# A recurrence in blocks of 24 steps, with the input products beside every step

## The reference, cut to what matters

```python
def cell(h, x):
    gi = x @ W_ih + b_ih
    gh = h @ W_hh + b_hh
    i_r, i_z, i_n = jnp.split(gi, 3, axis=-1)
    h_r, h_z, h_n = jnp.split(gh, 3, axis=-1)
    r = jax.nn.sigmoid(i_r + h_r)
    z = jax.nn.sigmoid(i_z + h_z)
    n = jnp.tanh(i_n + r * h_n)
    h_new = (1.0 - z) * n + z * h
    return (h_new, h_new)
```

## Time and profile before

| | us |
|---|---|
| median of 3 runs | 2068.12 (2065.51 to 2073.94) |
| the profiled execution | 2068.51 |
| its span in the profile | 2066.7 |
| TensorE busy | 1857.9 (90%) |
| recurrence: first gate matmul to the next stage's first matmul | 1138.73 to 2011.40 |

### The profile page before, as it was taken

One profiled execution on the slowest core, in us unless ns is written; L12 is line 12 of the kernel. 1 busy time (PEld: TensorE's weight loads), 2 busy tenths in 40 slices (PEclk: granted clock), 3 DMA queues, 4 the chain that ended last, 5 costly groups with the idle time before them and its releaser, 6 DMA issues. The chain is left out here.

```text
span 2066.7 us, 86137 instructions
## 1 busy us (share of the span) xinstructions
PE 1857.9 (90%) x32542; PEld 1377.3 (67%) x32542; DVE 1257.9 (61%) x5543; ACT 1097.8 (53%) x4105; POOL 377.3 (18%) x1398
## 2 busy tenths in 40 slices
PE   8877998999989989899888899999998999999876
PEld 4234454463644646455556898989898989999875
DVE  5545383654835447363343677777777777777766
ACT  0342736636355363645644565656565655656554
POOL 3000000000000000000000334343434333333335
PEclk7788999999999999999999796969797988879556
DMA  5222213222032220413223000000000000000002
GB/s 175 77 78 53 79 29 94 66 55 87 20 105 56 71 89 1 117 28 73 72 62 108 1 1 0 0 0 0 0 0 0 0 0 0 0 0 0 0 0 82
DMA packets 103527, 86.76 MB, mean 42 GB/s; under 512 B 15616, under 2 KB 90496, under 8 KB 103440
## 3 DMA queue, kind: packets, MB, share of 16 engines
q1 hardware_dynamic: 101392, 84.38, 14.2%
q10 hardware_dynamic: 1664, 1.18, 0.2%
q0 software_dynamic: 384, 0.01, 0.0%
HBM read 60.20 MB, written 21.00 MB: 39 GB/s over the span
## 5 line engine op out<-in xcount | busy, mean ns | idle before, releaser
L1255 PE MATMUL bank_pair_A<-moving,rep 128*128 128x16 f16 x8192 | 327.7, 172 | 55.3 <-DVE moving L1494 49.5
L1255 PEld LDWEIGHTS bank_pair_A<-moving,rep 128*128 128x128 f16 x8192 | 277.8, 99 | 75.6 <-DVE moving L1494 59.1
L1255 PE MATMUL bank_pair_C<-moving,rep 128*128 128x16 f16 x8192 | 321.8, 171 | 0.0
L1255 PE MATMUL bank_pair_B<-moving,rep 128*128 128x16 f16 x8192 | 321.7, 171 | 0.0
L1352 ACT ACTIVATE r_gate<-r_pre 128x16 f32<-128x16 f32 x512 | 110.4, 216 | 301.7 <-DVE r_pre L1443 301.7
L1255 PEld LDWEIGHTS bank_pair_C<-moving,rep 128*128 128x128 f16 x8192 | 266.3, 99 | 0.0
L1255 PEld LDWEIGHTS bank_pair_B<-moving,rep 128*128 128x128 f16 x8192 | 266.3, 99 | 0.0
L1242 PE MATMUL bank_pair_D<-x_part,w_in 128*128 128x256 f16 x1536 | 213.1, 288 | 6.0 <-ACT gi_rz L1379 3.5
L1443 DVE TENSOR_REDUCE r_pre<-bank_pair_A 128x16 f32<-128x32 f32 x512 | 98.1, 192 | 151.5 <-PE bank_pair_A L1255 151.5
L1137 POOL TENSOR_TENSOR x<-x,w_in 128x512 f32<-128x512 f32 x8 | 10.2, 1274 | 964.7 <-DMA w_in<-w_in 964.7
L1043 DVE TENSOR_REDUCE head_max<-bank_pair_A 128x2 f32<-128x1024 f32 x128 | 155.9, 1218 | 38.3 <-PE bank_pair_A L579 38.1
(11 more groups left out here) (260 smaller groups left out, 3632.0 us busy)
## 6 DMA issues: line engine op xcount, KB each, us to landing
rep<-parts SPq DMA_DIRECT2D x256, 64.0 KB
parts<-parts SPq DMA_DIRECT2D x48, 256.0 KB, 2.1
q_rep<-parts SPq DMA_DIRECT2D x32, 256.0 KB, 4.5
k_rep<-parts SPq DMA_DIRECT2D x64, 128.0 KB, 2.8
w_in<-in_x_dram SPq DMA_DIRECT2D x8, 512.0 KB, 4.2
x<-in_x_dram SPq DMA_DIRECT2D x8, 512.0 KB, 4.4
parts<-parts SPq DMA_DIRECT2D x32, 128.0 KB, 2.6
out_dram<-res SPq DMA_DIRECT2D x16, 256.0 KB, 2.1
```

Of the source, the lines that this page charges most:

```text
L1255: last = nc.tensor.matmul(ps[part][:, o:o + 2 * B], w[:, k, (first + c) * P:(first + c) * P + P], moving[j % 2][:, k, :, :].rearrange("p s ...
```

## The change

A block is now TS = 24 steps, which is exactly the 24 steps over which 12 groups spread; ten such blocks (FULL = 10) and 16 last steps (LAST = 16) make up the 256. Every step of the ten blocks carries a product: eight matmuls of 192 columns (24 tokens x 8) while the next block has 24 tokens, and of 128 columns in the tenth block, whose products are for the last 16 steps. Each step's product is followed by one matmul on constant operands (`steady`), 256 columns, into an otherwise unused bank; each of the last 16 steps, which have no product, is followed by eight of them. The split of x is made two blocks ahead, into one of two buffers chosen by the block's parity, in 8 pieces of 96 elements on the 16 r and z steps; the first two blocks' splits are made before the recurrence begins, on ScalarE and VectorE. GpSimd's wait for a moved n group remains once a block, behind the last group. The three inner loops run over groups 0 to 7, 8 to 10, and 11. The last two full blocks are written out after the outer loop of eight.

```diff
+    BODY = 2
+    TS = MC * BODY
+    FULL, LAST = N // TS, N % TS
...
-        x_part = t("x_part", [P, 2, DC, B, TB], F16)
+        x_part = t("x_part", [P, 2, 2, DC, B, TS], F16)
...
-        pG = [pD[:, 0, 0:B * TB], pD[:, 1, 0:B * TB]]
-        BLOCKS = N // TB
-        BODY = 2
-        PLAIN = TB - MC * BODY
+        pG = [pD[:, 0, 0:B * TS], pD[:, 1, 0:B * TS]]
...
+        def buffer_of(n):
+
+            return n % 2
+
+        def x_half(n, part, k, width):
+
+            return x_part[:, bass.ds(buffer_of(n), 1), part, :, :, :].rearrange("p o c b t -> p (o c) (b t)")[:, k, 0:B * width]
+
         def blocks(eng, step, product):
 
-
-            with eng.Fori(0, BLOCKS - 1) as blk:
-                with eng.Fori(0, PLAIN // BODY) as k:
-                    for j in range(BODY):
-                        step(blk * TB + k * BODY + j, j, blk, True, k)
-                with eng.Fori(0, RZ) as m:
-                    for j in range(BODY):
-                        step(blk * TB + m * BODY + (PLAIN + j), j, blk)
-                        product(blk + 1, m, j, False)
-                with eng.Fori(RZ, MC) as m:
-                    for j in range(BODY):
-                        step(blk * TB + m * BODY + (PLAIN + j), j, blk)
-                        product(blk + 1, m, j, True)
-            with eng.Fori(0, TB // BODY) as k:
+            def run(q, made, split):
+
+                for low, high in ((0, RZ), (RZ, MC - 1), (MC - 1, MC)):
+                    with eng.Fori(low, high) as m:
+                        for j in range(BODY):
+                            step(q * TS + m * BODY + j, j, (q + 2, m, split) if split and low == 0 else None)
+                            product(q + 1, m, j, (low >= RZ) + (high == MC), made)
+
+            with eng.Fori(0, FULL - 2) as q:
+                run(q, TS, TS)
+            run(FULL - 2, TS, LAST)
+            run(FULL - 1, LAST, None)
+            with eng.Fori(0, LAST // BODY) as k:
                 for j in range(BODY):
-                    step(k * BODY + (N - TB + j), j, BLOCKS - 1, True)
+                    step(k * BODY + (FULL * TS + j), j)
+                    product(FULL + 1, None, j, False, 0)
 
...
-            def products(m, k, bank):
+            def products(n, m, k, bank, width):
 
                 for w in range(2):
                     for part in range(2):
-                        last = nc.tensor.matmul(bank, w_in[w][:, k, bass.ts(m, P)], x_part[:, part, k, :, :].rearrange("p b t -> p (b t)"),
+                        last = nc.tensor.matmul(bank[:, 0:B * width], w_in[w][:, k, bass.ts(m, P)], x_half(n, part, k, width),
                                                 start=(k == 0 and w == 0 and part == 0), stop=(k == DC - 1 and w == 1 and part == 1))
                 return last
...
+            def steady(times):
+                for n in range(times):
+                    nc.tensor.matmul(pD[:, 1, 0:2 * P], w_in[0][:, n % DC, 0:P], w_in[1][:, n % DC, 0:2 * P], start=True, stop=True)
+
+            def product(n, m, j, is_n, width):
+                if not width:
+                    return steady(8)
                 if j == 0:
-                    pe.wait_ge(x_lo, blk * DC + DC)
-                    pe.wait_ge(gi_out, blk * MC + m)
+                    pe.wait_ge(x_lo, n * RZ + RZ)
+                    pe.wait_ge(gi_out, n * MC + m)
                 for k in range(j * DC // BODY, (j + 1) * DC // BODY):
-                    last = products(m, k, pG[0])
+                    last = products(n, m, k, pG[0], width)
                 if j == BODY - 1:
                     last.then_inc(gi_ps, 1)
+                steady(1)
...
-            for k in range(DC):
-                nc.scalar.activation(x_part[:, 0, k, :, :], xT[:, k, :, 0:TB], ACT.Copy).then_inc(x_hi, 1)
+            for n in range(2):
+                for k in range(DC):
+                    nc.scalar.activation(x_part[:, n, 0, k, :, :], xT[:, k, :, n * TS:(n + 1) * TS], ACT.Copy).then_inc(x_hi, 2)
...
-            def split(blk, k, j):
-
-                src = xT[:, bass.ds(k, 1), :, bass.ts(blk, TB)].rearrange("p o b t -> p (o b) t")
-                hi, lo = (x_part[:, n, bass.ds(k, 1), :, :].rearrange("p o b t -> p (o b) t") for n in range(2))
+            def split_of(n, m, width, j):
+
+                src = xT[:, :, :, bass.ds(n * TS, width)].rearrange("p c b t -> p (c b) t")[:, bass.ds(m * (B // 2), B // 2), :]
+                at = m // 2 * (B * TS) + buffer_of(m) * (B // 2 * width)
+                hi, lo = (x_part[:, bass.ds(buffer_of(n), 1), part, :, :, :].rearrange("p o c b t -> p (o c b t)")[:, bass.ds(at, B // 2 * width)]
+                          .rearrange("p (b t) -> p b t", b=B // 2) for part in range(2))
                 if j == 0:
                     nc.gpsimd.tensor_copy(hi, src).then_inc(x_hi, 1)
                 else:
-                    pool.wait_ge(x_hi, blk * DC + k + 1)
+                    pool.wait_ge(x_hi, n * RZ + m + 1)
                     nc.gpsimd.tensor_tensor(lo, src, hi, ALU.subtract).then_inc(x_lo, 1)
 
             def input_n(step):
...
-                if k is not None:
-                    split(blk + 1, k, j)
+                if split:
+                    split_of(*split, j)
...
-            def product(blk, m, j, is_n):
-                if j == BODY - 2 and is_n:
-
-                    pool.wait_ge(gi_out, blk * MC + m + 1)
+            def product(n, m, j, is_n, width):
+                if j == BODY - 2 and is_n == 2:
+
+                    pool.wait_ge(gi_out, n * MC + m + 1)
```

More of the change, by code:

```diff
@@ L1171, in recurrence @@
         bhh_c = t("bhh_c", [P, MC])
-        later = gi_rz[:, TB:N, :, :].rearrange("p t m b -> p (t m b)")
+        later = gi_rz[:, TS:N, :, :].rearrange("p t m b -> p (t m b)")
         staged = later[:, 0:DC * 3 * D].rearrange("p (c n) -> p c n", c=DC)
@@ L1294, in first_products @@
                     if m == 0:
-                        pe.wait_ge(x_lo, k + 1)
-                    last = products(m, k, pG[m % 2])
+                        pe.wait_ge(x_lo, 2 * (k + 1))
+                    last = products(0, m, k, pG[m % 2], TS)
                 last.then_inc(gi_ps, 1)
@@ L1344, in seed, with step @@
                                      src.unsqueeze(2).broadcast_to([P, c1 - c0, 2, B]), ACT.Copy).then_inc(seeded, 1)
-            def step(step, j, blk, begins=False, k=None):
+            def step(step, j, split=None):
                 def gate(kind, part):
@@ L1395, in _ @@
                     nc.scalar.activation(w_part[0][:, k, :], staged[:, k, :], ACT.Copy, scale=WS).then_inc(w_hi, 1)
-                evacuate(0, m, pG[m % 2], m >= RZ)
+                evacuate(0, m, pG[m % 2], m >= RZ, TS)
             act.wait_ge(begun, 1)
@@ L1405, in _ @@
         def _(dve):
-            for k in range(DC):
-                dve.wait_ge(x_hi, k + 1)
-                nc.vector.tensor_tensor(x_part[:, 1, k, :, :], xT[:, k, :, 0:TB], x_part[:, 0, k, :, :], ALU.subtract).then_inc(x_lo, 1)
+            for n in range(2):
+                for k in range(DC):
+                    dve.wait_ge(x_hi, n * RZ + 2 * (k + 1))
+                    nc.vector.tensor_tensor(x_part[:, n, 1, k, :, :], xT[:, k, :, n * TS:(n + 1) * TS], x_part[:, n, 0, k, :, :],
+                                            ALU.subtract).then_inc(x_lo, 2)
             dve.wait_ge(b_ld, 32)
@@ L1551, in step, with product @@
                 nc.gpsimd.tensor_tensor(tick[:, :], unit[:, 0, 0:1], unit[:, 0, 0:1], ALU.mult).then_inc(ticked, 1)
-                total = block_sums[:, :, :, bass.ds(blk, 1)].rearrange("p c b o -> p c (b o)")
+                total = block_sums[:, :, :, bass.ds(step // TB, 1)].rearrange("p c b o -> p c (b o)")
                 nc.gpsimd.tensor_tensor(total, total, xt, ALU.add).then_inc(summed, 1)
-            def product(blk, m, j, is_n):
-                if j == BODY - 2 and is_n:
-                    pool.wait_ge(gi_out, blk * MC + m + 1)
+            def product(n, m, j, is_n, width):
+                if j == BODY - 2 and is_n == 2:
+                    pool.wait_ge(gi_out, n * MC + m + 1)
             nc.gpsimd.memset(block_sums[:, :, :, :], 0.0).then_inc(summed, 1)
```

19 lines of the change are left out of this document (9 added, 10 removed).

## The result

| | before | changed |
|---|---|---|
| median, us (4 runs each, side by side) | 2070.69 (2065.51 to 2073.94) | 2216.53 (2214.86 to 2223.61) |
| the profiled execution | 2068.51 | 2216.85 |
| its span | 2066.7 | 2215.0 |
| recurrence: first gate matmul to the next stage's first matmul | 1138.73 to 2011.40, 872.7 | 1137.13 to 2162.62, 1025.5 |

Of the 148.3 us between the profiled executions the recurrence holds 152.8; what precedes it is 1.6 us shorter and what follows it 2.9.

What follows compares the result with a forecast made beforehand. TensorE was taken to bound steps with products, the chain over the engines plain steps. The profiled 2068.5 us + 146.9 for the steps - 2 - 1.5 for the edges gave 2211.9, named 2212; range 2040 to 2225.

Steps and rivals of the forecast that it cites:

- The likeliest case: Recurrence: half clock throughout the ten blocks, rising only in the last 16 steps; 2212 us, chance 0.48.
- The clock: Recurrence: starts at half clock and stays there through 216 steps and the tenth block; decides 0.77 us a step.
- The step at half clock: 216 steps with 192-column products: TensorE the only bound, 4.05 us each by scaling matmuls by columns, 874.8 in all.
- The block's end: Change of loops at a block's end: 0.30 us more than a step at full clock, hidden at half clock.
- The sum: All 256 recurrence steps: 1017.6 us against 870.7, +146.9; edges of -2 and -1.5 added to it.
- The first products: Before the recurrence: products 192 columns wide, 0.44 us less for each of four groups, -2 in all (0 to -4).
- what follows the recurrence: Next stage: starts at full clock if the last steps reach it, -1.5 us (0 to -8).
- The steps at full clock: Recurrence steps with products at full clock: 3.28 us on average, with 3.20 and 3.36 as ends.
- The first rival: Recurrence: full clock from the start or first steps, nearly throughout, 3.28 us a step; 2045 us, chance 0.25.
- 0.09 to 0.15 later: Every second step at full clock: delay in us from the loop's branch and six register instructions instead of four.
- the prediction's chain of 3.21: Step at full clock: VectorE's last split and the wait for the next sum limit it to 3.21 us, against TensorE's 3.17.
- Full clock at first, then lost: Recurrence: a block's end with its 0.30 us hole loses the clock after one to six blocks; 2100 to 2190, chance 0.14.

Runs made afterwards that it cites:

- Experiment 12: Changed kernel with all ten blocks written out, no outer loop, and a constant buffer number; start unchanged: 2212.68 us, ratio 1.070.
- experiment 11: Changed kernel with ten blocks written out, constant buffer number, one constant matmul per product, and twelve constant matmuls before step 0: 2038.33 us, ratio 0.986.
- 8: Changed kernel with two blocks written out in the outer loop's body, making the buffer's number a constant, nothing else: 2222.38 us.
- 2: Changed kernel without the one constant matmul behind each product; the eight a step in the last 16 steps stay: 2164.12 us.
- experiment 6: Changed kernel with two blocks written out in the outer loop's body, constant buffer number, and two or four constant matmuls per product: 2063.88 us, ratio 0.9975.
- experiment 3: Changed kernel with twelve constant matmuls of 256 columns in TensorE's wait before step 0, nothing else: 2209.67 us.
- 9: Changed kernel with ten blocks written out, constant buffer number, two to four constant matmuls per product, twelve more before the first step: 2044.46 us, ratio 0.989.
- 7: Changed kernel with two blocks written out in the outer loop's body, constant buffer number, and twelve constant matmuls before step 0: 2184.01 us.
- 4: Kernel before with eight constant matmuls behind each of its 88 steps without a product: 2051.97 us, ratio 0.990.
- 5: Kernel before with eight constant matmuls behind each of 88 plain steps, and GpSimd's wait only behind the last n group: 2044.64 us, ratio 0.990.
- 10: Kernel before with constants in its plain steps, GpSimd's wait only behind the last n group, and twelve constant matmuls at the start: 2087.64 us, ratio 1.010.

## Why the prediction came out

The likeliest case, half clock throughout with a chance of 0.48, was put at 2212 with its own range of 2195 to 2225; 2216.5 was measured. That narrow range is the test: the full one, 2040 to 2225, held nearly every case. The mechanism is the predicted one; that it was this case and not a rival was close to an even bet by the prediction's own chances.

**The clock, right.** The prediction took the start at half clock from the two waits around step 0, and held that steps with narrower products cannot raise it. Experiment 12 shows both with the changed kernel's own matmuls, and experiment 11, which fills the wait before step 0, starts at full. Experiments 8 and 2 show the second with two other steps. The sentence on what raises it is right too: out of eight constants of 256 columns it rose after three steps, as the prediction put it for the last 16, and the earlier trace rows showed before. The Trainium skill ("TensorE: Matmul & The Clock Gate", section on HAM oscillation) has idle gaps as what costs the clock. The runs agree where the idle time is long: the clock fell within the 3.60 us of experiment 6. They do not agree that nothing else costs it: it fell in experiment 3 with no idle time over 0.2 us in the 25 us before, and in experiment 11 where only the products became narrower. Nor is being busy enough for the rise: 890.00 us of 890.00 busy at 0.50 in experiment 3:

```profile
1210.00:2100.00 890.00, 890.00 (x23224) 855.86 (x23222) 536.88 (x3987) 464.65 (x2772) 293.42 (x1233) 0.50 0.00 0
```

**The step at half clock, right to 0.6%.** Put at 4.05, measured 4.05 and 4.10 in turn, 879.6 us for the 216 steps where the prediction had 874.8. The 4.05 is the scaling by columns. What the prediction put at nothing at half clock is the sequencer's work between product and next step, and that is the mis-sized term: with a constant buffer number (experiment 12) all product starts are 4.05 apart, a block takes 97.28 us between them, and the nine take 875.0 by GpSimd's marks, the predicted sum. In the changed kernel the eight blocks with the register take 97.8 to 97.9, and the ninth, which is written out and so has a constant, 97.28.

```profile
1297.56 1.44 PE L1253 MATMUL bank_pair_D<-x_part,w_in 128*128 128x192 f16 x8
...
1301.61 1.44 PE L1253 MATMUL bank_pair_D<-x_part,w_in 128*128 128x192 f16 x8
```

The block's end, put at nothing too, is nothing on TensorE: product starts 4.05 to 4.15 apart. The tenth block was put at 3.64 and took 3.62 by GpSimd's marks, 3.63 between product starts.

**The sum, short by 5 us in the profile.** +146.9 was predicted for the steps and -3.5 for the edges, 143.4; measured 152.8 and -4.5, 148.3. The 4.8 of the 216 steps are most of it. The first products were worth 1.6 us (put at 2), what follows the recurrence 2.9 (put at 1.5), though not by the way put, so that this term's size is luck: the clock fell 0.5 us into the next stage, at 2163.1, and was back at 2173.3, in time for these, which took 5.22 us before:

```profile
2172.58 3.15 PE L1659 MATMUL bank_pair_C<-block_sums,woT 128*128 128x64 f32 x24
```

**The steps at full clock, mis-sized.** The first rival's 3.28 with a register-addressed buffer was wrong: experiment 3 has 3.48. The failing term is "0.09 to 0.15 later" for the branch and six register instructions; in experiment 3 the sequencer needs 1.49 us in the median (1.43 to 1.63) from the product's first register instruction to the end of the next step's wait, 0.3 more than the 1.17 before. With a constant buffer product starts are most often 3.20 and 3.33 apart in r and z steps and 3.21 in n steps (experiment 11), 3.25 in the mean, as the prediction's chain of 3.21 and its ends 3.20 and 3.36 had it. The rival's 2045 is what experiments 9 (2044.5) and 11 (2038.3) reach, but they are other kernels: raising the clock at the start of the changed one (experiment 3) does not hold it.

**Full clock at first, then lost: real, with another trigger.** Experiment 3 loses it within the first block, not at its end, and the blocks' ends in experiments 9 and 11, with product starts up to 3.58 us apart, never lose it. That register addressing is what loses it in experiment 3 rests on the comparison of one run each of 3 and 7, and on 11; 7 and 11 hold it over the same steps; experiment 3 has TensorE busy 73.28 of its 75.00 full-clock microseconds, experiment 11 694.37 of 695.00:

```profile
1130.00:1205.00 75.00, 73.28 (x2054) 68.30 (x2052) 50.35 (x329) 41.35 (x237) 25.29 (x104) 1.00 0.00 1
```

No run of the register-addressed form without an outer loop was made, so the loops' part in it is not told apart.

**So where the gain went.** The change removes what made the clock dip (plain steps), worth 18 to 25 us as experiments 4 and 5 show with less. It also thins the steps with products, the only ones that raised it again, and the recurrence still starts low; so a possible gain of some 20 us became a loss of 146. Two faults lie on top of each other: with the start mended alone (experiment 3) the register-addressed steps lose the clock after 78 us, with the addressing mended alone (experiments 8 and 12) it never rises. Of the forms with one constant a product, only the one with both, and without a long jump back, holds it through nine blocks (experiment 11).

## What to carry to other kernels

When a change evens out TensorE's work, ask twice: does the new step hold a full clock, and would it raise a low one? Here the two answers differ, and then the level at which the long loop is entered decides over everything behind it, as long as nothing in the loop loses the clock. A few dense matmuls directly ahead of the loop were worth 173 us (experiments 11 and 12), but only 7 where the steps could not hold the clock (experiment 3), and where they made the jumps back long they cost 43 (experiments 5 and 10). A step's time at either clock can be read from rows of before by scaling its matmuls, but what stands between two matmuls on the sequencer must be counted too: 0.2 us a step at full clock here, 0.05 every second step at half. After any change of code length, look at the compare-and-branch rows of the outer loop: 0.2 us or 4.

## What was not expected of the hardware

- The same 256 steps ran in 840 us (experiment 11) or 1012 us (experiment 12) by the clock at their start, with TensorE busy nearly throughout in both.
- An outer loop's jump back cost TensorE's sequencer 3.4 to 4.8 us in four kernels (experiments 6, 7, 8, and five of six in 10) and 0.21 in others; twelve matmuls and a wait ahead of the loop turned one into the other (experiments 5 and 10).
- A moving operand whose buffer is chosen by a register made eight matmuls of 192 columns take 0.83 to 0.88 us to the next matmul on every second step at full clock (experiment 3), against 0.66 on every step with a constant buffer (experiment 11):

```profile
1209.16 0.82 PE L1253 MATMUL bank_pair_D<-x_part,w_in 128*128 128x192 f16 x8
1209.82 0.27 PE L1293 MATMUL bank_pair_D<-w_in 128*128 128x256 f16 x1
```
